# Attention with scaled fp16 queries and keys from the projections on, and the cast of the probabilities divided between ACT and GpSimd

## The reference

```python
c_kv, c_q = x @ w_dkv, x @ w_dq                  # 64 and 192 wide
k_r = rope((x @ w_kr))                           # 64 wide, shared by all heads
k_n = (c_kv @ w_uk).reshape(b, s, 16, 128)
q   = [rope(c_q @ w_qr), c_q @ w_uq]             # 64 + 128 wide per head
scores = einsum(q, [k_r, k_n]) / sqrt(192)
out = softmax(scores) @ (c_kv @ w_uv) @ w_o
x = layernorm(x + out)
x = layernorm(x + ffn(x))                        # silu(x @ w1q) * (x @ w3q) @ w2q, ternary weights
```

## Time and profile before

| what | value |
|---|---|
| median of 3 runs | 986.65 us (984.76 to 988.56) |
| profiled execution | 981.67 us |
| its span | 980.0 us, granted TensorE clock 0.989 |
| PE busy | 918.8 us, 94% of the span |
| DVE, ACT, POOL busy | 633.7, 680.4, 672.0 us (65%, 69%, 69%) |
| score matmuls (L1054) on the chain that ended last | Sa 14%, Sb 12% of the span |

### The profile page before, as it was taken

One profiled execution on the slowest core, in us unless ns is written; L12 is line 12 of the kernel. 1 busy time (PEld: TensorE's weight loads), 2 busy tenths in 40 slices (PEclk: granted clock), 3 DMA queues, 4 the chain that ended last, 5 costly groups with the idle time before them and its releaser, 6 DMA issues.

```text
span 980.0 us, 17588 instructions
## 1 busy us (share of the span) xinstructions
PE 918.8 (94%) x5110; PEld 637.5 (65%) x5110; DVE 633.7 (65%) x1008; ACT 680.4 (69%) x1140; POOL 672.0 (69%) x503
## 2 busy tenths in 40 slices
PE   6799899999999999979989989999999999998985
PEld 3558666666666666658776866666666666666874
DVE  1665677777776677744457667777777777773455
ACT  3735988888878888851334598888878888875132
POOL 0007788988888989760341778889898988875034
PEclk9999999999999999999999999999999999999998
DMA  9834798888787887999000579888787787889201
GB/s 254 260 156 113 141 167 156 147 152 152 150 155 144 152 152 145 160 177 346 16 25 23 129 140 165 149 156 158 144 159 148 147 152 150 151 155 194 118 1 43
DMA packets 419814, 142.24 MB, mean 145 GB/s; under 512 B 405596, under 2 KB 413616, under 8 KB 418736
## 3 DMA queue, kind: packets, MB, share of 16 engines
q1 hardware_dynamic: 418160, 131.11, 67.8%
q10 hardware_dynamic: 1024, 8.39, 2.2%
q0 software_dynamic: 576, 2.10, 0.6%
HBM read 24.38 MB, written 8.13 MB: 33 GB/s over the span
## 4 chain that ended last, share of the span: by engine, by line
PE 56%; issue 15%; ACT 10%; DVE 9%; POOL 5%; DMA 2%; ACTq 1%; DVEq 1%; POOLq 0%
PE Sa L1054 14%; PE Sb L1054 12%; PE Oa L1083 9%; DVE nmax L774 5%; ACT P_parts L451 3%; POOL P_parts L385 3%; ACT probs_a L552 3%; PE Sb L1107 2%; PE Tb L1065 2%; PE Sa L1107 2%; DMA Wvo_lo<-wvo_low 2%; POOL g_lo L427 2%; PE Ta L1065 1%; PE Ob L1093 1%; ACT PT_hi L451 1%
## 5 line engine op out<-in xcount | busy, mean ns | idle before, releaser
L385 POOL TENSOR_TENSOR P_parts<-probs_a,P_parts 128x768 f16<-128x768 f32 x128 | 211.5, 1652 | 43.3 <-ACT P_parts L451 42.1
L385 POOL TENSOR_TENSOR P_parts<-probs_b,P_parts 128x768 f16<-128x768 f32 x128 | 211.6, 1655 | 36.8 <-ACT P_parts L451 36.6
L774 DVE TENSOR_REDUCE nmax<-Sb 128x1 f32<-128x1024 f32 x128 | 156.8, 1225 | 58.2 <-PE Sb L1054 58.2
L774 DVE TENSOR_REDUCE nmax<-Sa 128x1 f32<-128x1024 f32 x128 | 154.8, 1210 | 37.8 <-PE Sa L1054 37.7
L1083 PE MATMUL Oa<-PT_dma,V_hi 128*64 128x512 f16 x768 | 132.3, 385 | 0.0
L552 ACT ACTIVATE probs_b<-Sa,nmax 128x1024 f32<-128x1024 f32 x64 | 71.3, 1114 | 68.4 <-DVE nmax L777 68.2
L361 POOL TENSOR_TENSOR turned<-qmul 128x1024 f32<-128x1024 f32 x16 | 38.1, 2402 | 104.0 <-DVE qmul L769 104.0
L451 ACT ACTIVATE P_parts<-probs_a 128x768 f16<-128x768 f32 x128 | 107.8, 842 | 0.4 <-DMA PT_dma<-P_parts 0.4
L451 ACT ACTIVATE P_parts<-probs_b 128x768 f16<-128x768 f32 x128 | 107.3, 840 | 0.0
L1054 PE MATMUL Sa<-K_hi,Q_hi 128*128 128x512 f32 x256 | 93.1, 445 | 10.0 <-ACT probs_b L552 9.3
L1054 PE MATMUL Sb<-K_hi,Q_hi 128*128 128x512 f32 x256 | 93.5, 446 | 7.2 <-ACT probs_a L552 4.5
(11 more groups left out here) (293 smaller groups left out, 1946.0 us busy)
## 6 DMA issues: line engine op xcount, KB each, us to landing
QO<-turned SPq DMA_DIRECT2D x64, 128.0 KB, 2.4
TT<-ternary SPq DMA_DIRECT2D x2, 2304.0 KB, 10.8
PT_dma<-P_parts SPq DMA_TRANSPOSE x256, 3.7
ternary<-tern ACTq DMA_DIRECT2D x1, 2304.0 KB, 8.2
wo<-in_L_attn_w_o_dram SPq DMA_DIRECT2D x4, 512.0 KB, 8.5
xq<-in_L_attn_x_dram SPq DMA_DIRECT2D x2, 1024.0 KB, 10.0
wq_high<-Wq_hi ACTq DMA_DIRECT2D x1, 2048.0 KB, 12.8
Wvo_lo<-wvo_low ACTq DMA_DIRECT2D x2, 1024.0 KB, 8.4
```

The costliest lines, as they stand in the source:

```text
L385: nc.gpsimd.tensor_tensor(P_parts[:, n % DEEP, 1, :], probs[n % DEEP][:, KP * P:S], P_parts[:, n % DEEP, 0, :], ALU.subtract).then_inc(par ...
L774: nc.vector.tensor_reduce(nmax[:, n % 4:n % 4 + 1], SS[n % 2][:, :], AX.X, ALU.max, negate=True).then_inc(row_max, 1)
```

## The change

K and all queries are held in fp16, as a high and a low part, scaled by powers of two. The factors k_up and q_up come from upper bounds: sums over the partitions of the largest |K| and of the largest latent times the largest weight, formed by a matmul with ones; exp takes the inverse, score_down, as its scale. QO as the store of queries is replaced by Q_parts [128, 16, 2, 1024] in fp16. Queries are split as they leave the projections: ACT the high, DVE (latent rows) and GpSimd (rotary rows) the low parts; latent copies are full-height, and SP moves the upper half of one head to the other by a DMA. The per-pair split on GpSimd is gone. The cast of the 6 blocks of the probabilities is divided: ACT casts the last four, GpSimd the first two. Wq_hi stays in place for the whole kernel; all of Wq_lo goes to DRAM and its place holds Wvo_lo and xr during the attention, loaded by SP ahead of the first transpose of a batch. The values are turned in group 1 in place of group 0.

```diff
+            def latents_high(g, i):                                      # ACT
+                act_.wait_ge(k_step, b * KSTEPS + 18)
+                act_.wait_ge(q_ps, b * 4 * GROUPS + 4 * g + 3 + i)
+                for n in range(2):
+                    scaled(Q_parts[:, 4 * g + 2 * i + 1, 0, n * HALF:(n + 1) * HALF], (TS, OS)[i][n][:, :], q_up)
+            def rotary_parts_high(g, j):                                 # ACT
+                act_.wait_ge(rope_sum, b * 2 * GROUPS + 2 * g + j + 1)
+                if g >= 1: act_.wait_ge(turned_out[j], b * 64 * GROUPS + 64 * g)
+                copy(turned_parts[:, j, 0, :], turned[:, j, :])
...
                     nc.scalar.activation(probs[n % DEEP], SS[n % 2][:, :], ACT.Exp, bias=nmax[:, n % 4:n % 4 + 1],
+                                         scale=score_down,
...
-                    copy(P_parts[:, n % DEEP, 0, :], probs[n % DEEP][:, KP * P:S])
+                    copy(P_parts[:, n % DEEP, 0, 2 * P:KD * P], probs[n % DEEP][:, (KP + 2) * P:S])
...
+                def low_probs(tile, n, reused):                          # GpSimd
+                    hold(pool, exp_done, EXP0 + tile + 1)
+                    if reused is not None: hold(pool, part_in[n % DEEP], reused)
+                    nc.gpsimd.tensor_scalar(P_parts[:, n % DEEP, 0, 0:2 * P], probs[n % DEEP][:, KP * P:(KP + 2) * P],
+                                            1.0, 1.0, ALU.mult, ALU.mult)
+                    hold(pool, part_cast, tile + 1)
                     hold(pool, part_hi, tile + 1)
                     nc.gpsimd.tensor_tensor(P_parts[:, n % DEEP, 1, :], ..., ALU.subtract)
...
+                    for j in range(2):                                   # GpSimd, each group
+                        pool.wait_ge(rope_hi, b * 2 * GROUPS + 2 * g + j + 1)
+                        nc.gpsimd.tensor_tensor(turned_parts[:, j, 1, :], turned[:, j, :], turned_parts[:, j, 0, :], ALU.subtract)
...
+                for j in range(2):                                       # SP, after the projections
+                    sp.wait_ge(turned_out[j], (b + 1) * 64 * GROUPS)
+                sp.wait_ge(q_ps, (b + 1) * 4 * GROUPS)
+                sp.dma_start(Wvo_lo[...], wvo_low).then_inc(wvo_in, 16)
+                sp.dma_start(xr[:, :, :], x_v[b]).then_inc(xr_in, 16)
                 with sp.Fori(0, PAIRS) as p:                             # the transposes follow
...
+                for g in range(GROUPS):                                  # DVE
+                    rotate(g)                                            # four of L769, now times q_up as well
+                    latents_low(g, 0)                                    # two of 128x512
+                    if g == 0: K_lo, after k_hi
+                    if g == 1: V_lo, after v_hi
+                    if g < GROUPS - 1: latents_low(g, 1)
...
                         if g == 1 and j == 3:                            # TensorE
+                            turn_values()
+                            pe.wait_ge(cq_lod, b * 4 + 4)                # V_lo
...
-                    nc.vector.tensor_scalar(nmax[...], nmax[...], PROB_UP_LOG, None, ALU.add)
+                    nc.vector.tensor_scalar(nmax[...], nmax[...], score_down, PROB_UP_LOG, ALU.mult, ALU.add)
...
-                    for k, (w, c) in enumerate(((Q_hi, K_hi), (Q_hi, K_lo), (Q_lo, K_hi))):
+                    for k, (part, c) in enumerate(((0, K_hi), (0, K_lo), (1, K_hi))):     # all fp16
```

More of the change, by code:

```diff
@@ L93, in build @@
             ("Wq_hi", [P, H, 2, P], R), ("Wq_lo", [P, H, 2, P], R))
[L95 to L98, removed]
+        (Wvo_lo, xr), AT = lay(
+            K_AT - H * 2 * P * 4, ("Wvo_lo", [P, PAIRS, D], R), ("xr", [P, QT, D], F))
+        assert AT <= K_AT
+        (K_hi, K_lo, V_hi, V_lo, vscale, limits, ffs, minus_half, nmax, den, rden, rden_wide, rden_row, stats, mv, ve,
          rstd), QO_AT = lay(
-            K_AT, ("K_hi", [P, S], R), ("K_lo", [P, S], R),
+            K_AT, ("K_hi", [P, S], F16), ("K_lo", [P, S], F16),
             ("V_hi", [P, KT, KVR], F16), ("V_lo", [P, KT, KVR], F16),
-            ("vscale", [P, 4], F),
+            ("vscale", [P, 4], F), ("limits", [P, 16], F),
             ("ffs", [P, 8], F),
@@ L319, in _ @@
                 sp.wait_ge(part_lo, (b + 1) * TILES * PAIRS + DEEP)
+                for r in range(DEEP):
+                    sp.wait_ge(part_in[r], 16 * (b + 1) * (TILES * PAIRS // DEEP))
                 sp.dma_start(TT[:, :].bitcast(F), ternary).then_inc(tt_in, 16)
                 if b + 1 < B:
[L322 to L326, removed]
+                    sp.wait_ge(att_ps, (b + 1) * QT)
+                    sp.wait_ge(att_res, b * 48 + 24)
+                    sp.dma_start(Wq_lo[:, :, :, :].rearrange("p h c m -> p (h c m)").bitcast(F), wq_low).then_inc(wq_in, 16)
         @block.gpsimd
@@ L343, in _ @@
             with pool.Fori(0, B) as b:
[L344 to L353, removed]
+                nc.gpsimd.memset(ones_b[:, :], 1.0).then_inc(ones_ready, 1)
                 for g in range(GROUPS):
@@ L386, in low_probs, with pair_pool @@
                                             P_parts[:, n % DEEP, 0, :], ALU.subtract).then_inc(part_lo, 1)
-                def pair_pool(p, first, last):
+                def pair_pool(p, first):
                     pair = b * PAIRS + p
@@ L391, in pair_pool @@
                         h = n // 8
-                        low_probs(pair * TILES + n, n)
+                        low_probs(pair * TILES + n, n,
+                                  None if first and n < DEEP else 16 * (pair * TILES // DEEP + n // DEEP))
                         if n % 8 == 0 and not (first and h == 0):
@@ L396, in pair_pool @@
                             low_out(pair * 2 + h - 2, p * 2 - 2, h)
[L397 to L413, removed]
+                pair_pool(0, True)
+                with pool.Fori(1, PAIRS) as p:
+                    pair_pool(p, False)
                 widen(b * PAIRS * 2 + 2 * PAIRS - 1, 1)
@@ L602, in pair_act @@
                             exponent(t0 + n + 1, n + 1)
-                        else:
-                            act_.wait_ge(scores_ready, b * TILES * PAIRS + TILES * PAIRS)
-                            act_.dma_start(Wvo_lo[:, :, :].rearrange("p j d -> p (j d)").bitcast(F),
-                                           wvo_low).then_inc(wvo_in, 16)
-                        if first and n == 8:
-                            act_.wait_ge(lat_out, b * 8 * GROUPS + 8 * GROUPS)
-                            for j in range(2):
-                                act_.wait_ge(turned_out[j], b * 64 * GROUPS + 64 * GROUPS)
                         part_high(t0 + n, n, None if first and n < DEEP else 16 * (t0 // DEEP + n // DEEP))
@@ L815, in pair_dve @@
                             transposed_low(pair * (TILES // 2) + n // 2, n)
-                for n in range(2):
-                    maximum(b * PAIRS * TILES + n, n)
+                maximum(b * PAIRS * TILES, 0)
+                latents_low(GROUPS - 1, 1)
+                maximum(b * PAIRS * TILES + 1, 1)
                 dve.wait_ge(rope_sum, b * 2 * GROUPS + 2 * GROUPS)
@@ L1034, in turn_values @@
                 def turn_values():
[L1035 removed]
+                    hold(pe, k_step, b * KSTEPS + 19)
                     for k in range(KT):
[L1037 removed]
+                        last = nc.tensor.transpose(Oa[:, k * KVR:(k + 1) * KVR], kmul[64:128, k * P:(k + 1) * P],
                                                    ident[64:128, 64:128])
```

253 lines of the change are left out of this document (157 added, 96 removed).

## The result

The changed kernel takes 1006.1 us (median, 1003.0 to 1006.4) against 987.6 (984.8 to 995.1) before on the same chip: ratio 1.017, 95% interval 1.011 to 1.023. The profiled executions have spans of 1004.2 and 980.0.

The account below looks back on a forecast made before the run. TensorE's own sum and a scores-maximum-exp-cast chain both lie within 0.5 us of the period. Terms -13.5 +16 +17 -6.3 -1.1 = +12 us: 994 from the profiled 981.7, 998 from the median 986.65; range 974 to 1016.

Parts of the forecast that it names:

- the half clock: TensorE, idle long behind the queue wait, may return at the lower granted clock: up to 2 us, left in the range.
- The steady half-pair: Attention loop: shorter scores and cast, longer exp and maximum step; period 20.4, 0.45 less for 30 half-pairs, -13.5 us.
- 2 sets of scores in the chain: Loop's chain: one period holds two sets of fp16 scores, 1.35 for 1.50 us each, giving 0.30.
- the cast: ACT's cast in the loop, 768 to 512 columns: three on the chain give 0.66 us a half-pair.
- the second step: Second step of the maximum on DVE, scale from an SBUF operand: 0.05 us more, three times, 0.15 a half-pair.
- The pointer: Exp's scale from an SBUF operand: 0.09 us more each, four on the chain, 0.34; bounds 0 and 0.09 each.
- GpSimd: GpSimd's list in a half-pair: 18.6 becomes 19.5 of 20.4 us, not the bound; bounds 18.9 and 21.3.
- Rival (c): Loop: GpSimd becomes the bound, half-pair 21.3, total 1023 us; deciding point 0.50 for the cast; chance 0.13.
- The start of a batch: Work ahead of exp 1: later rotation, late V_lo idling TensorE 4.9, longer ACT copies; +8.0 a batch, +16; bounds 4 and 11.
- The SP queue: Wvo_lo and xr loads ahead of the first transpose hold ACT's cast of tile 4: +8.4 a batch, +17; bounds 2.6 and 11.
- What goes: End of a batch: TensorE's waits of 3.61 and 2.66 us for Wvo_lo vanish, -6.3 us.
- The prologue: Very start: ACT issues one DMA less, 1.22 us, ahead of its table load and first copies; -1.1 us.

Follow-up runs that it names:

- e_cast_act: The changed kernel with the divided cast alone undone, ACT casting all six blocks and GpSimd none: 1025.5 us, ratio 1.037.
- e_const: The changed kernel with a constant in place of the scale pointer in exp and the maximum's second step, true scale left out: 990.9 us, half-pair 20.17.
- e_score2: The changed kernel without the product of high queries and low keys, one of three score products: 992.8 us, half-pair 20.15.
- e_const_ahead: The changed kernel with the constant scale (true scale left out) and GpSimd's cast issued one tile ahead: 995.6 us, half-pair 19.90.
- e_three_ahead: The changed kernel with three cast blocks each on ACT and GpSimd, and GpSimd's cast one tile ahead: 998.3 us, ratio 1.012, half-pair 20.24.
- e_v: The changed kernel with V_hi ahead of group 1's latent high parts on ACT and V_lo behind the second of group 1's rotation products on DVE: 997.5 us, ratio 1.010.
- e_best_max: e_best with the second tile's maximum on DVE put ahead of the low parts of the last latents: 978.2 us.
- the two load variants: The changed kernel with the Wvo_lo and xr loads issued behind pairs' transposes: in eighths, pairs 0 to 7, 1008.9 us; in quarters, pairs 0 to 3, 993.6 us.
- e_best: The changed kernel with e_v, e_spread4 and e_three_ahead together: 978.4 us, ratio 0.991 to the kernel before.
- e_spread4: The changed kernel with the Wvo_lo and xr loads issued in quarters behind the 16 transposes of pairs 0 to 3: 993.6 us, ratio 1.005.

## Why the prediction was right, and where it was not

The side, the mechanisms that were named and the range (974 to 1016) were right; the size was short by 8 us on the medians (998 against 1006), by 12 on the profiles. By the rows of the table, most of the 12 is the start of the batches (7.2 in both), where the half clock was put at nothing. The queue adds 2.2, and the prologue 3.3, which these runs cannot pin on the change. The rows of the loop (+2.5) and of the end (-3.1) nearly cancel; 1.7 of that is only that four half-pairs are counted in the last row.

- **The steady half-pair.** Forecast 20.4 and -0.45; measured 20.45 and -0.42. Its terms: scores started 0.22 apart and the set took 1.31 (forecast 1.35), exp +0.09 as forecast, the cast 0.62 a half-pair (0.66), the second step +0.06 (0.05). e_cast_act shows the cast's term, and its 0.62 fits three casts (840 less 625 ns each, 0.65). e_const and e_score2 show that exp and scores count, by at least 0.27 and 0.29 before GpSimd stops them. The 0.55 of e_const_ahead fits 4 exps and 3 second steps (0.54). That there are 2 sets of scores in the chain was only argued and stays so, and the 0.21 of e_three_ahead does not fit three casts.
- **The pointer.** The Trainium skill ("ScalarE: Activation LUTs", What ACT_TABLE_LOAD costs) has 93 ns for each per-partition pointer operand; exp went from 1115 to 1205 ns, 90 for the second pointer. The measurement agrees.
- **GpSimd.** Forecast 19.5, measured 20.15: cast 0.40 (0.39), but 0.68 from the cast's start to the low part's, where 0.59 was set. Rival (c), GpSimd as the bound, was 0.3 us away, though its deciding point (0.50 for the cast) was not reached.
- **The start of a batch, mis-sized.** Forecast 8.0, with bounds of 4 and 11; measured 11.6 in both batches, outside them. How much later than before TensorE is (batch 0, less the 2.2 of the prologue) grows in steps. At the first set of group 1 it is 1.1, by the longer scaling steps (1.3 forecast). The idle of 1.65 ahead of that set is not a further term: TensorE comes to it 0.6 sooner than before, as the values are no longer turned in group 0. At the fourth set it is 7.1 (6.7 forecast), by 0.2 of slow first matmuls, 0.8 for turning the values here and the idle of 5.0 (4.9). Up to here the forecast holds. Then comes the step that failed: the half clock, 2.6, was put at nothing here; the forecast names a lower clock for the idle in the queue alone, and leaves it in the range there. The next sets add 0.1. The forecast's last 1.3 (8.0 less 6.7, ACT's longer copies) became 1.7: 0.7 before the first exp and 1.0 between the first and second, by DVE's and ACT's order. 1.1 + 0.2 + 0.8 + 5.0 + 2.6 + 0.1 + 1.7 = 11.5. e_v shows 5.0 of it by experiment. The last 1.7 is read from the trace alone; e_best_max shows that it is not DVE's order alone.
- **The SP queue.** Forecast 8.4, measured 10.5 and 8.7; the loads alone 6.8 to 8.6 by the two load variants. What is left over (1.9 to 3.7 in batch 0, 1.3 to 1.5 in batch 1) holds the late end of the turned queries, and the half clock of the window at 140; the runs do not part the two. The forecast's own sum does not close: 116.4, eight issues of 0.67 and a landing of 2.4 are 124.2 and not 122, and 122 with 8 and with 2 to 3 is 132 to 133 and not 131.5. Counted from the second exp the loads were issued 9.0 behind it by the forecast and 8.4 in the trace; from there to ACT's cast it set 9.5, and it took 11.6 (127.25 to 138.85) and 10.1 in batch 1. So the mis-sized term is what the loads and the first transpose take.
- **What goes.** The waits for Wvo_lo are gone: in after no Wvo_lo matmul has idle before it. The stretch holds the last two half-pairs too, so -4.7 a batch is -3.1 and two times -0.42, with 0.7 open.
- **The prologue.** Forecast -1.1, measured +2.2. In the windows of after, 50 to 55 and 55 to 60 us had a granted clock of 0.54 and 0.77, before 0.66 and 1.00; and the landmark behind it wanders by 10 us over the profiles of variants that share this code. So the removed ACT issue can't be seen, and the +2.2 is no effect that these runs can pin on the change.

## What to carry to other kernels

Ask of every transfer moved to an earlier place what stands behind it in its queue: 2 MB that nobody needed for 300 us cost 7 to 9 us a batch at the head of a queue of transposes, and nothing that the half-pair shows in quarters behind them (but the last part must not end up behind the last of them). When a chain is shortened, sum every engine's list of the period first; the next limit here was 0.3 us away, and two different cuts ended at 20.17 and 20.15. And price an idle of TensorE of some 5 us with the half-clock stretch behind it, here 2.6 us on top of 5.0.

## What the runs showed of the hardware

- After idles of 5.0 and 10.1 us TensorE came back at 0.52 and 0.50 of its clock (1.2 of 2.4 GHz), with matmuls 0.43 apart. The idle of 5.0 stands in nine of the profiles, in both batches, and all 18 times the half clock followed.
- A shorter idle is not safe. After one of 1.57 to 1.59 us the clock was full five times out of six and half once (e_best, batch 0). After one of 4.11 us in e_spread4 the first matmuls ran at full clock and the next at half:

```profile
137.28 0.61 PE L1111 MATMUL Sa<-K_hi,Q_parts 128*128 128x512 f16 x2 [4.11 <-ACT probs L574]
137.72 0.59 PE L1111 MATMUL Sa<-K_lo,Q_parts 128*128 128x512 f16 x2
138.15 0.95 PE L1111 MATMUL Sa<-K_hi,Q_parts 128*128 128x512 f16 x2
```

- GpSimd's copy to fp16 with two scalar operands takes 0.40 us for 256 and 0.51 for 384 columns of 128 partitions; by these two points, an estimate, some 0.19 of it is fixed. An operation that waits for the one just ahead of it on GpSimd starts 0.28 us behind its end.
- The fp16 weight loads of the scores take 98 ns, the fp32r ones took 188, yet the set of six matmuls fell by 0.19 only (1.50 to 1.31).
